# A product of the state-space loop, formed by VectorE from a second softplus in PSUM in place of GpSimd

## The reference, cut to what matters

```
u, z = split(seq @ W_in.T);  u = silu(causal_conv4(u) + conv_b)      # 128 channels each
x_dbl = u @ W_x.T                                                    # 4 + 16 + 16 columns
dt = softplus(x_dbl[:4] @ W_dt.T + b_dt);  B, C = the other 16 + 16
h[t] = exp(dt * A) * h[t-1] + (dt * u) * B[t]                        # for each of 16 states
y = sum over states of h * C + u * Dp
out = (y * silu(z)) @ W_out.T
```

## Time and profile before

| | |
|---|---|
| time, median of 3 runs | 5542.64 us (5542.42 to 5544.48) |
| the profiled execution, its own time | 5538.76 us |
| its span, first to last instruction | 5537.0 us, granted TensorE clock 0.966 of full |
| busy, share of the span | PE 90%, DVE 83%, POOL 81%, ACT 63%, PEld 48% |
| first drive of chunk 0, first drive of chunk 63 | 54.86 us, 3332.99 us |
| last scan of the loop, last gate | 3381.79 us, 3388.57 us |

### The profile page before, as it was taken

The page is one execution under the profiler, slowest core; times in us unless marked ns, Lnnn a source line. Parts: engine busy times, 40 slices in busy tenths (PEclk is TensorE's granted clock), DMA queues, the critical chain, the costliest instruction groups (busy, mean ns, idle before and its releaser), DMA issues. The chain is left out here.

```text
span 5537.0 us, 68281 instructions
## 1 busy us (share of the span) xinstructions
PE 4966.8 (90%) x22742; PEld 2647.6 (48%) x22742; DVE 4575.0 (83%) x6402; ACT 3477.0 (63%) x4188; POOL 4496.1 (81%) x2067
## 2 busy tenths in 40 slices
PE   7999999999999999999999997882769999999998
PEld 3444444444444444444444444530546666666666
DVE  8999999999999999999999997104878778688665
ACT  5666676676676676666666663000658777777776
POOL 6999999999999999999999996001557777677776
PEclk9999999999999999999999999796889999999999
DMA  5666666666666666666666663493789999999999
GB/s 206 211 216 215 215 215 217 213 213 214 216 215 213 214 219 213 214 216 213 214 219 212 213 219 112 190 401 90 155 155 199 198 198 197 198 197 199 198 199 187
DMA packets 1416309, 1137.13 MB, mean 205 GB/s; under 512 B 1212666, under 2 KB 1222546, under 8 KB 1408532
## 3 DMA queue, kind: packets, MB, share of 16 engines
q1 hardware_dynamic: 1411480, 1131.52, 74.7%
q10 hardware_dynamic: 4478, 1.25, 0.2%
HBM read 814.23 MB, written 21.09 MB: 151 GB/s over the span
## 5 line engine op out<-in xcount | busy, mean ns | idle before, releaser
L822 POOL TENSOR_TENSOR mamba_state<-mamba_state,mamba_c_row 128x1024 f32<-128x1024 f32 x1024 | 2397.8, 2364 | 59.1 <-DVE mamba_state L795 54.5
L693 PE MATMUL mamba_y_ps<-mamba_state,ident 128*128 128x512 f32 x4096 | 1959.9, 604 | 123.6 <-POOL mamba_state L822 119.3
L795 DVE TENSOR_TENSOR_SCAN mamba_state<-mamba_decay,mamba_b_ps 128x1024 f32<-128x1024 f32 x704 | 1609.8, 2287 | 94.6 <-ACT mamba_b_ps L771 1.0
L1957 POOL TENSOR_TENSOR l3s_el<-l3s_s_sb,l3s_eh 128x1024 f16<-128x1024 f32 x512 | 1088.7, 2149 | 424.0 <-ACT l3s_s_sb L1942 209.3
L693 PEld LDWEIGHTS mamba_y_ps<-mamba_state,ident 128*128 128x128 f32 x4096 | 758.7, 190 | 943.3 <-issue 674.1
L1965 DVE TENSOR_SCALAR_CACHE_REDUCE l3s_s_sb<-l3s_s_ps 128x512 f32<-128x512 f32 x1024 | 685.7, 687 | 245.3 <-PE l3s_s_ps L1898 239.5
L1912 PE MATMUL l3s_o_ps<-l3s_vt,l3s_et 128*128 128x257 f16 x4096 | 808.9, 276 | 58.1 <-DMA l3s_et<-l3s_el 25.0
L781 DVE TENSOR_TENSOR mamba_b_ps<-mamba_dtu,mamba_b_ps 128x1024 f32<-128x1024 f32 x704 | 849.5, 1207 | 4.6 <-PE mamba_b_ps L681 4.5
L1941 ACT ACTIVATE l3s_eh<-l3s_s_sb,l3s_shift 128x1024 f16<-128x1024 f32 x512 | 583.8, 1140 | 375.9 <-issue 170.3
L771 ACT ACTIVATE mamba_decay<-mamba_dt,mamba_A 128x1016 f32<-128x1016 f32 x704 | 783.0, 1134 | 4.1 <-DVE mamba_state L795 0.2
L816 POOL TENSOR_TENSOR mamba_b_row<-mamba_b_row,mamba_dtu 128x1024 f32<-128x1024 f32 x320 | 756.4, 2364 | 0.2 <-DMA mamba_b_row<-mamba_c_rows 0.2
(11 more groups left out here) (325 smaller groups left out, 5247.0 us busy)
## 6 DMA issues: line engine op xcount, KB each, us to landing
mamba_c_row<-mamba_c_rows SPq DMA_DIRECT2D x1024, 512.0 KB, 3.9
mamba_b_row<-mamba_c_rows SPq DMA_DIRECT2D x320, 512.0 KB, 5.5
l_ring_a<-in_L_conv_W SPq DMA_DIRECT2D x28, 1024.0 KB, 11.0
l2b_ring_b<-in_L_conv_W SPq DMA_DIRECT2D x26, 1024.0 KB, 11.0
l_ring_a<-in_L_conv_W SPq DMA_DIRECT2D x14, 704.0 KB, 12.7
l2b_ring_b<-in_L_conv_W SPq DMA_DIRECT2D x13, 704.0 KB, 12.7
l_ring_a<-in_L_conv_W SPq DMA_DIRECT2D x14, 640.0 KB, 12.1
l2b_ring_b<-in_L_conv_W SPq DMA_DIRECT2D x13, 640.0 KB, 12.1
```

What stands on the lines that cost most here:

```text
L693: last = nc.tensor.matmul(y_ps[:, half(h)], C["ident"][:, :], state[:, s % STATES, half(h)], start=False, stop=(s == S - 1))
L795: nc.vector.tensor_tensor_scan(state[:, s % STATES, :], by, add, 0.0, ALU.mult, ALU.add).then_inc(s_scan, 1)
L822: nc.gpsimd.tensor_tensor(state[:, s % STATES, :], state[:, s % STATES, :], c_row[:, s % C_ROWS, :], ALU.mult).then_inc(s_hc, 1)
L1957: nc.gpsimd.tensor_tensor(el[:, part, off:off + EXPW], s_sb[:, par, j * EXPW:(j + 1) * EXPW], eh[:, part, off:off + EXPW], ALU.subtract).t ...
```

## The change

The product dtu leaves pool_prep (k = 13, reading dt from SBUF) and goes to a new dve_prep at k = 9, which reads it from PSUM: ACT, behind the Softplus that writes dt into SBUF, runs the same Softplus again and writes it over prep_ps in place. pe_prep's product for z, which overwrites prep_ps, moves from k = 10 to k = 11 and waits for dtu in place of dt; silu(z) moves from k = 11 to k = 12. dve_prep is the first thing in dve_unit, and in chunk 0's own preparation it is called behind the statistics of each k. The diff is whole:

```diff
--- before.py
+++ after.py
@@ -564,6 +564,7 @@
         s_cw = sem(f"{tag}_c_written")
         s_pdt = sem(f"{tag}_dt_matmul")
         s_dt = sem(f"{tag}_dt_ready")
+        s_dt_ps = sem(f"{tag}_dt_in_psum")
         s_dtu = sem(f"{tag}_dtu_ready")
         s_pz = sem(f"{tag}_z_product")
         s_sz = sem(f"{tag}_silu_z_ready")
@@ -664,8 +665,8 @@
                 for h in range(2):
                     last = nc.tensor.matmul(prep_ps[:, half(h)], weights(n)["w_dt"][:, :], u[:, par, half(h)], start=True, stop=True)
                 last.then_inc(s_pdt, 1)
-            if k == 10:
-                wait(pe, s_dt, n + 1)
+            if k == 11:
+                wait(pe, s_dtu, n + 1)
                 for h in range(2):
                     nc.tensor.matmul(prep_ps[:, half(h)], weights(n)["w_z"][rows(h), :], xt[rows(h), :],
                                      start=True, stop=True).then_inc(s_pz, 1)
@@ -740,9 +741,11 @@
                 wait(act, s_decay, S * (n - 1))
                 nc.scalar.activation(dt[:, par, :], prep_ps[:, :], ACT.Softplus,
                                      bias=weights(n)["b_dt"][:, 0:1]).then_inc(s_dt, 1)
+                nc.scalar.activation(prep_ps[:, :], prep_ps[:, :], ACT.Softplus,
+                                     bias=weights(n)["b_dt"][:, 0:1]).then_inc(s_dt_ps, 1)
                 act.preload_act_table_set(EXP_LN_TABLES)
 
-            if k == 11:
+            if k == 12:
                 wait(act, s_pz, 2 * n + 2)
                 wait(act, s_yz, n - 1)
                 nc.scalar.activation(sz[:, par, :], prep_ps[:, :], ACT.Silu).then_inc(s_sz, 1)
@@ -772,6 +775,14 @@
                                  scale=weights(c)["A"][:, s:s + 1]).then_inc(s_decay, 1)
 
 
+        def dve_prep(dve, n, par, k):
+            if k == 9:
+                wait(dve, s_dt_ps, n + 1)
+                wait(dve, s_u, n + 1)
+                wait(dve, s_drive, len(DVE_UNITS) * (n - 1))
+                wait(dve, s_bdrive, len(POOL_UNITS) * (n - 1))
+                nc.vector.tensor_tensor(dtu[:, par, :], prep_ps[:, :], u[:, par, :], ALU.mult).then_inc(s_dtu, 1)
+
         def dve_drive(dve, c, par, s):
             if s in POOL_UNITS:
                 return
@@ -800,14 +811,6 @@
             wait(dve, s_out, c)
             nc.vector.tensor_tensor(yz[:, :], sz[:, par, :], y_ps[:, :], ALU.mult).then_inc(s_yz, 1)
 
-        def pool_prep(pool, n, par, k):
-            if k == 13:
-                wait(pool, s_dt, n + 1)
-                wait(pool, s_u, n + 1)
-                wait(pool, s_drive, len(DVE_UNITS) * (n - 1))
-                wait(pool, s_bdrive, len(POOL_UNITS) * (n - 1))
-                nc.gpsimd.tensor_tensor(dtu[:, par, :], dt[:, par, :], u[:, par, :], ALU.mult).then_inc(s_dtu, 1)
-
         def pool_drive(pool, c, par, s):
             if s == POOL_UNITS[0]:
                 wait(pool, s_dtu, c + 1)
@@ -881,6 +884,8 @@
                 act_add(act, c - 1)
 
         def dve_unit(dve, c, par, s, prep):
+            if prep:
+                dve_prep(dve, c + 1, 1 - par, s)
             dve_drive(dve, c, par, s)
             if s == GATE_AT and not is_first(c):
                 dve_gate(dve, c - 1, 1 - par)
@@ -890,8 +895,6 @@
             late = behind(c, par, s, 1)
             if late:
                 pool_product(pool, *late)
-            if prep:
-                pool_prep(pool, c + 1, 1 - par, s)
             if s + DRIVE_AHEAD in POOL_UNITS:
                 pool_drive(pool, c, par, s + DRIVE_AHEAD)
             pool_norm(pool, c, s)
@@ -936,6 +939,7 @@
                     if k in SECOND_STATS:
                         dve.wait_ge(s_x[SECOND_STATS[k]], 16)
                         norm.vector_stats(dve, SECOND_STATS[k])
+                    dve_prep(dve, 0, 0, k)
                 run(dve, dve_unit)
                 dve_gate(dve, LAST, LAST % 2)
 
@@ -946,8 +950,6 @@
                 for slot in range(DECAYS):
                     nc.gpsimd.memset(decay[:, slot, :].rearrange("p (q t) -> p q t", t=T)[:, :, 0:1],
                                      0.0).then_inc(s_zero, 1)
-                for k in range(S):
-                    pool_prep(pool, 0, 0, k)
                 run(pool, pool_unit)
                 pool_product(pool, LAST, LAST % 2, S - 1)
```

## The result

| | before | changed |
|---|---|---|
| median us (range) | 5543.24 (5542.42 to 5544.48), 4 runs | 5577.26 (5574.45 to 5578.46), 4 runs |
| ratio | | 1.0057, 95% interval 1.0042 to 1.0072 |
| first drive | 54.86 | 68.00 |
| first drive to last scan | 3326.9 | 3344.4 |
| last scan to last gate | 6.8 | 6.8 |

The lower rows are of the two profiled executions (spans 5537.0 and 5576.6). Slower by 34 us in the medians. The profiled executions differ by 39.6 us: 13.1 ahead of the first drive, 17.4 in the loop, 9.1 behind the last gate, where no code differs.

What follows compares the result with a forecast made beforehand. DVE and POOL, each needing about 51.0 us a chunk in one ring, bound the loop, DVE alone after the change; 8.6 (loop) + 11.5 (start) + 20 (clock falls) = +40 us, giving 5582, range 5557 to 5610.

Steps and rivals of the forecast that it cites:

- POOL's relief removes the gate's wait: State-space loop, DVE's gate at unit 2: without dtu on POOL its idle goes, up to 1.0 us a chunk.
- DVE's product costs 1.14 and is not hidden: Loop, before drive 9: DVE's need rises from 51.03 to 52.17 us a chunk; loop +8.6 us net.
- ACT at 0: Loop, units 8 to 9: second softplus takes 1.1 us without a table load, hidden with 0.9 us to spare: 0.
- PE's z and Silu at 0: Loop, units 11 to 12: z and Silu one unit later fit existing gaps, with 3.4 us of cover: 0.
- Falls of the clock: Loop, PE's idle at unit 12 grows to 2.8 us; TensorE's clock falls in 40 of 62 chunks: +20 us.
- the 0.5 a fall: Loop, drive 15: each clock fall costs 0.5 us, from 1.7 us of lost PE work against 1.3 of slack.
- The start: First preparation: statistics of images 2 and 3 queue behind DVE's wait for both softplus; first drive at 66.4, +11.5 us.
- Behind the loop: Stages after the loop's last gate: no term in the forecast's sum, so 0.
- the rival of a clean DVE bound: Loop: clock falls cost nothing as slack takes them; +20 us in all, 5563 us; chance 0.24.

Runs made afterwards that it cites:

- e4: Kernel before, with POOL's product dtu cut to 16 of 1024 columns in all chunks but the first two: 5484.1 us, ratio 0.9898.
- e5: Changed kernel, with POOL still forming the old product at unit 13 into a tile nobody reads: 5611.5 us, ratio 1.0127.
- e6: Kernel before, with ACT's second softplus into PSUM added and POOL still forming dtu from SBUF: 5558.4 us, ratio 1.0037.
- e3: Changed kernel, with PE's two matmuls of z at k = 11 done twice: 5570.7 us, ratio 1.0054.
- e7: Changed kernel, with six and not five states multiplied by POOL (units 2, 4, 7, 9, 12, 14): 5503.8 us, ratio 0.9933.
- e9: Changed kernel measured again, unaltered: 5580.6 us, ratio 1.0063.
- e11: Changed kernel, with six POOL units at 2, 5, 7, 10, 12, 14 and statistics of images 2 and 3 moved earlier: 5565.0 us, ratio 1.0033.

## Why the prediction was right, and where it was off

The forecast was 5582 and slower; measured 5577.3. The mechanism held, and one term, the price of the clock's falls, was twice too large. By its steps:

- *POOL's relief removes the gate's wait*: right, 0.0 us in 63 gates, and e4 and e5 show it from both sides. On the way I counted 15 gates of the kernel before as delayed by a fall; the trace has 13, and others idle for 0.8 to 0.9 us without one.
- *DVE's product costs 1.14 and is not hidden*: right. 1.20 us of instruction, 1.12 of progress, period 52.13 where the sum gave 52.17. A loop of 63 x 52.14 is +6.7 us where 8.6 was said.
- *ACT at 0*: right in the changed kernel, with the load and the time as said (1.08). But the cover (0.9 us said, 1.0 measured) was DVE's own delay (e6).
- *PE's z and Silu at 0*: right.
- *Falls of the clock*: the place and the number were right (2.4 to 2.6 us of idle for 2.8 worked out, 41 falls for 40), the price was not: +20 said, 9 measured (e3). That the number came so close is luck: 40 of 62 was a choice, worked out from no row. The mis-sized term is the 0.5 a fall. I let each take 1.7 us from PE against 1.3 of slack. In the chunk shown the rows and the sum behind the idle take 1.22 + 2.85 for 0.73 + 1.88, 1.5 us, and the rows of unit 15 are done at 1527.72, still 0.42 us before drive 15 starts at 1528.14. Only the five falls of double length cost their period 1.2 to 1.5 us (such as that before 1894.96), and the others 0.1 on average: DVE waits for PE's rows 10 times, 8.3 us.
- *The start*: +11.5 said, 13.1 measured. The order was right; ACT's first Softplus came at 50.28 and not 48.48 because PE's product for u took 6.49 us against 5.13 and that for dt 3.78 against 3.01, at a low clock in a different part of the preparation. First drives of the later kernels with the same order of statistics and both softplus (e3, e5, e7, e9) lie from 67.07 to 68.60. So 1.5 us of this term is scatter, but all lie above the 66.4 said. The stall of 2 us that I left out of the sum did not come.
- *Behind the loop*: 0 said. Of the medians' 34 us, 3.4 are neither in the start nor in the loop, within the 20 us by which that part varies.

The total looks better than its parts, and that is luck. The falls were 11 us too large and the loop 1.9; against them stand 1.6 at the start, 1.7 of other waits in the loop, and 3.4 outside both. So the forecast is off by 5 us and not by 13. The truth lies between my forecast and the rival of a clean DVE bound (5563): the falls cost something, but half of what I gave them.

## What to carry to other kernels

Where two engines in a ring need the same time, neither's busy share tells what moving an instruction brings: add up what each needs by itself, start to start, and compare the larger sum with the present period; here 52.17 against 52.03 said the move could not win, and that a drive handed back to POOL could (50.7 and 51.0, and 0.8% faster). Such a sum is a floor and not a forecast: e11 has the same two needs and a period of 52.23, because one drive came too late for its scan. Price a fall of TensorE's clock by the slack behind it, too: 1.8 us where the gate waited for PE (before), 0.2 where PE's rows had slack before their drive (changed). Count in the program's start too: an instruction put in an in-order list makes all behind it wait for its operands, and once cost 10 us that a reordering of the list gave back. A margin holds only in the kernel in which both of its sides were read.

## What the runs showed of the hardware

- A fp32 product of 128x1024 with both inputs in SBUF took 1.22 us on DVE with POOL idle (one instruction) and 1.44 in the median beside POOL, whose own product beside it took up to 3.36 instead of 2.37; with one input in PSUM it took 1.20 and POOL showed nothing. The Trainium skill (GPSIMD Engine Reference, Specifications) names two SBUF inputs as a case of contention; the trace agrees and gives the price for both sides.
- Softplus on ACT from PSUM to the same place in PSUM took 1.08 us, behind another Softplus without a table load.
- Two idles of PE of nearly the same length, 2.36 and 2.55 us, in neighbouring chunks: with the shorter the clock was halved for 3.4 us, with the longer it was not. Over the loops, idles before unit 12 of 1.5 to 1.7 us came with no fall (before, e3), one of 1.97 with a fall (e3), and those of 2.4 to 2.8 with a fall in 41 of 62 chunks (changed); idles of 1.75 to 2.0 before sum 13 with 13 in 54 (before).
